# A fused decoder layer: q and k by tiles of 128 tokens across batch borders, with the engines' orders written out

## The chip, the cores and the metric

One core of a Trainium2 chip runs the whole layer in one launch. The metric is the device time of that launch in microseconds. The core has five engines that run beside each other and meet at semaphores: TensorE (PE, matmuls), VectorE (DVE), ScalarE (ACT), GpSimd (POOL) and SyncE (SP), which here only issues DMAs.

## The reference

32 batches of T = 112 tokens, model width M = 256, H = 8 heads of D = 128, a context of S = 375 rows per batch, FFN width F = 1024. Cut to what matters:

```
def attn(x, wq, wk, wv, wo):                     # x is layer-normed
    q, k, v = (einsum('bim,mhd->bhid', x, w) for w in (wq, wk, wv))
    q, k = rope(rmsnorm(q)), rope(rmsnorm(k))    # per head, over d
    s = (q * mult) @ (k * mult).T - 1e30 * later_keys
    return einsum('bhid,hdm->bim', softmax(s) @ v, wo)

x = x + attn(layernorm(x), wq, wk, wv, wo)
x = x + gelu(layernorm(x) @ ctx.T) @ ctx         # context of its own for each batch
x = x + quantised_ffn(layernorm(x), w1, b1, w2, b2)
```

The q and k projections treat each token by itself; only the rotary table depends on a token's place in its batch. Scores need all of a batch's q and k with D on the partitions.

## The kernel before

A batch's 112 tokens sit on 112 partitions. Each engine runs one loop, `body(i)`, whose order of work is written by hand; batches are pipelined over its iterations, so that one body of PE projects batch i+3, scores i+2 and finishes i-3.

The path of one batch's q and k: `stats_x`, `normalise_x` (DVE) and `root_x` (POOL) give the normed rows; `round_xn` (ACT) and `split_xn` (DVE) give them as a high and a low half in fp16; `transpose_x` (SP, a DMA transpose) puts M on the partitions. `project_q` and `project_k` (PE) do 12 matmuls each of 512 columns (two chunks of M, high x high, high x low, low x high, two banks), `project_v0` and `project_v1` 6 each. `square_q`, `square_k` (ACT) and `sum_squares_*` (DVE) give the RMS sums, `turn_cos_*`, `turn_sin_*` (DVE, straight from PSUM) the two products of the rotation, added by `turn_q` (DVE) and `turn_k` (POOL). ACT's `round_q0/1` scales and rounds q's high half, and `split_q` (DVE) makes its low half, one instruction per head:

```
for h in range(H):
    last = dve.scalar_tensor_tensor(out=qk16[:, 0, 1, at], in0=turn_c[:, 0, at], scalar=rms[:, 0, h:h + 1],
                                    in1=qk16[:, 0, 0, at], op0=ALU.mult, op1=ALU.subtract)
```

k goes by `scale_k0/1` and `round_k0` (ACT) and `split_k` (DVE). `transpose_q` and `transpose_k` (SP) each move 112 x 2048 fp16 values to `qkT`. Then `scores` (PE), `softmax_exp` (ACT), `mask_later_keys` (POOL), `weigh_values` (PE, P times V with a column of constants that gives the row sums), `invert_sums` (DVE), `normalise_o0/1`, `round_o` (ACT), `split_o` (DVE), `transpose_o` (SP), `project_out0` to `3` (PE), the residual, and the context and FFN parts in the same manner (`ctx_hidden`, `ctx_out`, `hidden_units0/1`, `out_units` on PE).

SP's queue holds every DMA of the kernel in one order; a wait in it holds back all that follow. PSUM has eight banks, and all are shared in turn: q's banks 3 and 4 also take part of o, k's banks 0 and 1 the scores.

## Time and profile before

| | us |
|---|---|
| three runs, median | 654.1 |
| three runs, lowest and highest | 652.81, 654.41 |
| the profiled execution | 654.7 |
| its span in the profile | 652.9 |
| of the span, PE busy | 593.3 |
| DVE busy | 588.1 |
| ACT busy | 543.0 |
| POOL busy | 348.0 |

The span runs from the first instruction of the program to the last; the time is what the device reports for the launch. Busy time of an engine counts each moment once, though its instructions overlap a little at their ends.

### The profile page before, as it was taken

To read this page: it belongs to the slowest core of one execution; us is meant where nothing else is said; L and a number is where in the kernel's file an instruction comes from. 1 tells how busy PE (TensorE), PEld (TensorE's weight loads), DVE (VectorE), ACT (ScalarE), POOL (GpSimd) and SP (SyncE) were. 2 spreads that over 40 slices of the span, in tenths; PEclk is the share of its full clock that TensorE was granted. 3 is DMA by queue.
4 is the path that set the end of the run, shared out by engine and by line. 5 is a ranking of instruction groups with operands and counts; after the bars stand their busy time and mean duration, and the time that the engine had idled before them with its cause. 6 is when DMAs were issued, how large, how long until landed. Compare 5 with 4: busy or idle time off the path is not lost.

```text
span 652.9 us, 13103 instructions
## 1 busy us (share of the span) xinstructions
PE 593.3 (91%) x4624; PEld 477.3 (73%) x4624; DVE 588.1 (90%) x1339; ACT 543.0 (83%) x1402; POOL 348.0 (53%) x430
## 2 busy tenths in 40 slices
PE   1746889999999999999999999999999999997864
PEld 1424667777887788888778877888887788776753
DVE  3768899999999999999999999999999999998442
ACT  6675788999999999989998899999889999998522
POOL 1134555665555565666655555656666555556111
PEclk9967999999999999999999999999999999999978
DMA  8071566766776766667687676666677777666451
GB/s 296 0 200 36 114 139 138 137 138 150 149 148 137 147 133 142 141 141 153 133 151 152 143 152 138 137 142 132 143 149 138 150 152 146 134 141 138 89 109 37
DMA packets 222641, 88.92 MB, mean 136 GB/s; under 512 B 200704, under 2 KB 217552, under 8 KB 222320
## 3 DMA queue, kind: packets, MB, share of 16 engines
q1 hardware_dynamic: 222576, 88.08, 63.6%
q8 instruction: 37, 0.61, 0.4%
q14 instruction: 28, 0.23, 0.1%
HBM read 34.84 MB, written 3.67 MB: 59 GB/s over the span
## 4 chain that ended last, share of the span: by engine, by line
DVE 75%; ACT 9%; PE 5%; POOL 3%; issue 3%; DMA 3%; SPq 0%; ACTq 0%; DVEq 0%
DVE turn_s L433 11%; DVE turn_c L425 8%; DVE qk L524 8%; DVE o L550 5%; DVE ss L566 5%; DVE turn_c L614 5%; DVE ss L603 5%; DVE qk L639 4%; DVE h_t L590 2%; DVE y_out L545 2%; DVE g L628 2%; DVE x L634 2%; DVE stat L534 1%; POOL turn_c L354 1%; DVE xn L600 1%
## 5 line engine op out<-in xcount | busy, mean ns | idle before, releaser
L912 PE MATMUL psum<-wqkv,xT 128*112 128x512 f16 x384 | 148.3, 386 | 12.5 <-DMA xT<-xn 9.1
L913 PE MATMUL psum<-wqkv,xT 128*112 128x512 f16 x384 | 147.4, 384 | 0.0
L914 PE MATMUL psum<-wqkv,xT 128*112 128x512 f16 x384 | 147.1, 383 | 0.0
L354 POOL TENSOR_TENSOR turn_c<-turn_c,turn_s 112x1024 f32<-112x1024 f32 x32 | 75.7, 2365 | 48.4 <-DVE turn_s L433 48.4
L912 PEld LDWEIGHTS psum<-wqkv,xT 128*112 128x112 f16 x384 | 50.7, 132 | 43.4 <-DMA xT<-xn 9.7
L425 DVE TENSOR_TENSOR turn_c<-psum,cos_t 112x1024 f32<-112x1024 f32 x64 | 77.8, 1215 | 0.0
L433 DVE TENSOR_TENSOR turn_s<-psum,sin_t 112x1024 f32<-112x1024 f32 x64 | 77.7, 1214 | 0.0
L914 PEld LDWEIGHTS psum<-wqkv,xT 128*112 128x112 f16 x384 | 50.7, 132 | 34.1 <-issue 1.9
L922 PE MATMUL psum<-wo,oT 128*112 128x256 f16 x256 | 71.0, 277 | 4.7 <-DMA oT<-o 3.5
L524 DVE SCALAR_TENSOR_TENSOR qk<-turn_c,rms,qk 112x128 f16<-112x128 f32 x256 | 69.2, 343 | 2.6 <-ACT qk L796 2.5
L924 PE MATMUL psum<-wo,oT 128*112 128x256 f16 x256 | 71.0, 277 | 0.0
L923 PE MATMUL psum<-wo,oT 128*112 128x256 f16 x256 | 71.0, 277 | 0.0
L913 PEld LDWEIGHTS psum<-wqkv,xT 128*112 128x112 f16 x384 | 50.7, 132 | 27.6 <-issue 1.3
L385 POOL TENSOR_TENSOR ve<-mv,ln_eps 112x1 f32<-112x1 f32 x32 | 6.6, 205 | 109.1 <-DVE mv L518 109.1
L1051 PE MATMUL psum<-v_sb,p_sb 112*112 112x129 f32 x512 | 62.1, 273 | 0.5 <-DVE turn_s L433 0.5
L1051 PEld LDWEIGHTS psum<-v_sb,p_sb 112*112 112x112 f32 x512 | 58.9, 176 | 0.9 <-POOL p_sb L368 0.9
L346 POOL TENSOR_TENSOR x3b<-x,b_rows 112x256 f32<-112x256 f32 x32 | 48.3, 1509 | 16.5 <-DVE y_out L545 13.2
L362 POOL TENSOR_TENSOR rms<-ms,nhalf 112x8 f32<-112x8 f32 x32 | 55.1, 1723 | 2.5
L381 POOL TENSOR_TENSOR rms<-ms,nhalf 112x8 f32<-112x8 f32 x32 | 53.3, 1665 | 2.5
L341 POOL TENSOR_TENSOR ve<-mv,ln_eps 112x1 f32<-112x1 f32 x32 | 9.2, 287 | 81.0 <-DVE mv L537 81.0
L1013 PE MATMUL psum<-qkT 128*112 128x112 f16 x256 | 42.6, 218 | 10.0 <-DVE turn_s L433 9.7
L961 PE MATMUL psum<-ctx_in,g 125*112 125x256 f32 x192 | 48.6, 390 | 3.3 <-ACT v_sb L708 3.3
(107 smaller groups left out, 1699.2 us busy)
## 6 DMA issues: line engine op xcount, KB each, us to landing
ctxT<-in_ctx_cols SPq DMA_DIRECT2D x32, 375.0 KB, 3.4
ctx_in<-in_ctx_rows SPq DMA_DIRECT2D x32, 375.0 KB
x_in<-in_x SPq DMA_DIRECT2D x32, 112.0 KB, 2.3
out_y<-y_out SPq DMA_DIRECT2D x32, 112.0 KB, 2.9
w_raw<-in_w SPq DMA_DIRECT2D x2, 1024.0 KB, 6.1
w_raw<-in_wk SPq DMA_DIRECT2D x2, 512.0 KB, 5.0
w_raw<-in_wq SPq DMA_DIRECT2D x2, 512.0 KB, 6.5
w_raw<-in_wv SPq DMA_DIRECT2D x2, 512.0 KB, 8.2
```

What stands on the lines that cost most here:

```text
L354: pool.tensor_tensor(turn_c[:, 1, :], turn_c[:, 1, :], turn_s[:, 1, :], ALU.add).then_inc(k_turned, 1)
L362: pool.tensor_tensor(rms[:, 1, :], ms[:, 1, :], nhalf[0:T, 0:H], ALU.pow).then_inc(k_rms_done, 1)
L425: return dve.tensor_tensor(turn_c[:, w, :].rearrange("t (b h d) -> t b h d", b=2, d=D), ps.rearrange("t b (h d) -> t b h d", d=D), cos_t[: ...
L433: return dve.tensor_tensor(turn_s[:, w, :].rearrange("t (h two f) -> t h two f", two=2, f=HALF), halves, table, ALU.mult)
L524: last = dve.scalar_tensor_tensor(out=qk16[:, 0, 1, at], in0=turn_c[:, 0, at], scalar=rms[:, 0, h:h + 1], in1=qk16[:, 0, 0, at], op0=ALU.m ...
L912: pe.matmul(dst, hi, wqkv[:, 0, c, w, cols], start=c == 0, stop=False)
L913: pe.matmul(dst, hi, wqkv[:, 1, c, w, cols], start=False, stop=False)
L914: last = pe.matmul(dst, lo, wqkv[:, 0, c, w, cols], start=False, stop=c == MC - 1)
L922: pe.matmul(y_ps, oT16[:, h, :], wo16[:, 0, h, :], start=first and h == heads[0], stop=False)
L923: pe.matmul(y_ps, oT16[:, h, :], wo16[:, 1, h, :], start=False, stop=False)
L924: product = pe.matmul(y_ps, oT16[:, H + h, :], wo16[:, 0, h, :], start=False, stop=last and h == heads[-1])
L1051: last = pe.matmul(o_ps[:, h // OH, at:at + VW], p_sb[:, h * T:(h + 1) * T], v_sb[:, h, :], start=h % OH == 0, stop=h % OH == OH - 1 or h ...
```

## The change

Eight batches of 112 tokens are 896 = 7 x 128 tokens. q and k are computed for 28 tiles of 128 consecutive tokens, whatever batch they belong to, in place of 32 batches of 112. A group is eight batches and seven tiles; `has_tile()` is false for every eighth batch, and in its place nothing of the x, q and k path is issued. Tile j of a group holds the last 112 - 16 j rows of batch j first (`own_rows`), then the first rows of batch j + 1. So `transpose_q` moves the rows of batch j to their place in `qkT`, and `transpose_q_next` the rest to the other buffer, in one DMA or two (`pieces_after`: a piece begins at partition 0, 32, 64 or 96, and rows that it takes too many land in a pad of 16 columns); k likewise. `qkT` has two buffers, `xT16` holds a group of seven tiles, the rotary tables have a row per token of a group (the cosine one only half as wide), and x is loaded a second time by tiles (`load_rows`). v is still projected per batch, now in the body of its scores (`project_v0/1` on columns of `xT16` that can lie in two tiles). q's low half is still made head by head from the rotated q, for 28 tiles. Some buffers share their room (`kn` with the raw weights, `on` and `p_sb` with the raw wo), and the PSUM banks are given out anew. Weights are prepared in another order, with a semaphore for each.

The order of each engine is new. It is now a `start()` and an `end()` of single calls and a `body(i)` for i = 5 to 25 between them.

```
+def done_t(j):
+    return (GROUP - 1) * (j.off // GROUP) + min(j.off % GROUP + 1, GROUP - 1)
...
+    def own_rows(j):
+        own = (P - T) * (j.off % GROUP)
+        return own, T - own
+    def pieces_after(cut):
+        a = cut // 32 * 32
+        return ((32, 64), (64, P)) if a == 32 else ((a, P),)
...
-                sp.dma_start_transpose(qkT[:, 0], qk16[:, 0].rearrange("t l n -> t (l n)")).then_inc(qT_landed, 16)
+                sp.wait_ge(q_lo_done, done_t(j))
+                own, cut = own_rows(j)
+                sp.dma_start_transpose(qkT[:, j.off % 2, 0, :, PAD + own:PAD + T], qk16[0:cut, 0].rearrange("t l n -> t (l n)")).then_inc(qT_landed, 16)
+            def transpose_q_next(j):
...
+                for a, b in pieces_after(cut):
+                    sp.dma_start_transpose(qkT[:, (j.off + 1) % 2, 0, :, PAD + a - cut:PAD + b - cut],
+                                           qk16[a:b, 0].rearrange("t l n -> t (l n)")).then_inc(qT_next_landed, 16)
...
-            def turn_cos(w, ps):
+            def turn_cos(w, ps, r):
+                table = cos_t[:, r, :].unsqueeze(1).broadcast_to([P, 2 * H, HALF])
...
-            def project(w, n, dst, j):
+            def project(w, n, dst, cols_of_x):
...
-                    hi, lo = xT16[:, c, :], xT16[:, MC + c, :]
+                    hi, lo = xT16[:, c, cols_of_x], xT16[:, MC + c, cols_of_x]
...
+            def scores(j):
+                pe.wait_ge(kT_landed, 16 * done_t(j))
+                pe.wait_ge(qT_landed, 16 * done_t(j))
...
+                if j.has(1):
+                    pe.wait_ge(qT_next_landed, next_landed(j.plus(-1)))
...
             def body(i):
-                a, b, c, d, e, f, g = (Batch(i + 3), Batch(i + 2), Batch(i + 1), Batch(i - 0), Batch(i - 1), Batch(i - 2), Batch(i - 3))
...
+                b, d, f, g, h = (Batch(i + 2), Batch(i - 0), Batch(i - 2), Batch(i - 3), Batch(i - 4))
+                project_out1(f)
+                project_out2(f)
+                project_out3(f)
+                project_out0(f)
+                project_v1(d)
+                ctx_out(g)
+                if b.has_tile():
+                    project_k(b)
+                hidden_units0(h)
+                scores(d)
+                project_v0(d)
+                transpose_xn2(f)
+                hidden_units1(h)
+                if b.has_tile():
+                    project_q(b)
+                ctx_hidden(f)
+                weigh_values(d)
+                out_units(h)
```

DVE's body of the change runs one place ahead of PE's (its g is i-3 where PE's f is i-2). On DVE the place is in the middle of the run, around the two products of k's rotation (`turn_c<-psum,cos_t` at L425, the first of the two, and `turn_s<-psum,sin_t`). Before, in every body:

```order
L550 TENSOR_TENSOR o<-on,o 112x1024 [waits o_hi_done]
L425 TENSOR_TENSOR turn_c<-psum,cos_t 112x1024 [waits k_squared]
L433 TENSOR_TENSOR turn_s<-psum,sin_t 112x1024
L563 SCALAR_TENSOR_TENSOR x<-psum,x 112x256 [waits x3b_done,ctxout_ready]
L566 TENSOR_REDUCE ss<-sq 112x8
L425 TENSOR_TENSOR turn_c<-psum,cos_t 112x1024 [waits q_squared]
L576 TENSOR_SCALAR xn<-x_in,mv,rstd 112x256 [waits x_rstd_done]
L581 BN_STATS stat<-x 112x6 [waits x3_done]
```

And now, in a group's seventh body (i = 6, 14, 22), where the tile whose k would be turned is missing:

```order
L848 TENSOR_TENSOR turn_c<-turn_c,turn_s 128x1024 [waits q_cos_done,q_sin_done]
L852 TENSOR_SCALAR xn<-x,mv,rstd 112x256 [waits x2_rstd_done]
L856 TENSOR_TENSOR qk<-w_raw,qk 128x1024 [waits k_hi0_done]
L860 TENSOR_SCALAR xn<-x_rows,mv,rstd 128x256 [waits x_rstd_done]
L874 BN_STATS stat<-x 112x6 [waits x3_done]
L876 MEMSET wait_cell 1x1 [waits x3_bn_done]
L877 BN_AGGR mv<-stat 112x2
L879 TENSOR_SCALAR ve<-mv 112x1 [waits x3_mv_done]
L895 TENSOR_SCALAR f_q<-f_int 128x448 [waits f0_int_done]
L900 TENSOR_SCALAR xq_int<-x,mv,rstd 112x256 [waits x3_rstd_done]
L904 TENSOR_SCALAR f_q<-f_int 128x448 [waits f1_int_done]
```

In a body with all tiles, k's sum of squares (L865), its sine product (L758) and its cosine product (L751) stand between `xn<-x_rows` and the statistics at L874 and behind them; they are gone from this body, q's sum of squares too, while q's addition (L848) and k's low half (L856) are still there. These two, with q's products and q's low half, are missing in the body after it.

On SP's queue, before, one body of the middle of the run (`qkT<-qk` is k's transpose at L266 and q's at L275, `oT<-o` is o's):

```order
L266 DMA_TRANSPOSE qkT<-qk 128x16x112 [waits k_lo_done]
L271 DMA out_y<-y_out 112x256
L275 DMA_TRANSPOSE qkT<-qk 128x16x112 [waits q_lo_done]
L279 DMA_TRANSPOSE oT<-o 128x16x112 [waits o_lo_done]
L282 DMA ctx_in<-in_ctx_rows 125x768
L289 DMA_TRANSPOSE xT<-xn 128x4x112 [waits v1_ready,xn_lo_done]
L250 DMA ctxT<-in_ctx_cols 128x2x375
L255 DMA_TRANSPOSE xqT<-xq 128x2x112 [waits xq_done]
```

And now, in a group's fifth body (k of tile 5 at L359 and L367 in the end of it, q of tile 4 at L329 and L337):

```order
L318 DMA_TRANSPOSE xqT<-xq 128x2x112 [waits xq_done]
L323 DMA ctxT<-in_ctx_cols 128x2x375 [waits h_ready]
L329 DMA_TRANSPOSE qkT<-qk 128x16x48 [waits q_lo_done]
L337 DMA_TRANSPOSE qkT<-qk 128x16x32 [waits q_lo_done]
L337 DMA_TRANSPOSE qkT<-qk 128x16x64
L343 DMA ctx_all<-in_ctx_rows 125x768 [waits ctxout_ready]
L348 DMA out_y<-y_out 112x256 [waits out_done]
L354 DMA_TRANSPOSE oT<-o 128x16x112 [waits y0_added,o_lo_done]
L359 DMA_TRANSPOSE qkT<-qk 128x16x32 [waits k_lo_done]
L367 DMA_TRANSPOSE qkT<-qk 128x16x32 [waits k_lo_done,s_ready]
L367 DMA_TRANSPOSE qkT<-qk 128x16x64
```

Between two context loads there stood two transposes for q and k, and there are now six, the last of them 16 to 64 rows wide; a store now waits for its result before o's transpose can be issued.

## Rows read from the trace of the kernel before

**Rows 1.** The page: busy us, share of the span and instructions of each engine.

```profile
PE 593.3 (91%) x4624; PEld 477.3 (73%) x4624; DVE 588.1 (90%) x1339; ACT 543.0 (83%) x1402; POOL 348.0 (53%) x430
```

**Rows 2.** Windows: us; busy PE, PEld, DVE, ACT, POOL; PEclk; DMA share; GB/s.

```profile
0.00:113.80 113.80, 74.41 (x463) 53.02 (x464) 86.20 (x160) 81.02 (x170) 45.97 (x64) 0.93 0.53 132
113.80:580.60 466.80, 466.35 (x3747) 379.32 (x3746) 462.30 (x1066) 424.02 (x1121) 281.48 (x338) 1.00 0.69 143
580.60:614.50 33.90, 29.37 (x248) 24.78 (x246) 25.10 (x65) 24.35 (x67) 14.53 (x17) 0.95 0.69 138
614.50:652.90 38.40, 23.20 (x175) 20.18 (x172) 14.55 (x50) 13.65 (x47) 6.07 (x11) 0.83 0.29 65
```

**Rows 3.** Timeline of PE, one body: start us, us, what it does.

```profile
302.12 0.21 PE L1013 MATMUL psum<-qkT 128*112 128x112 f16 x1
...
305.95 0.27 PE L922 MATMUL psum<-wo,oT 128*112 128x256 f16 x1
...
308.57 1.94 PE L1051 MATMUL psum<-v_sb,p_sb 112*112 112x129 f32 x16
310.35 1.04 PE L938 MATMUL psum<-w2T,f_q 128*112 128x256 bf16 x8
311.22 0.38 PE L912 MATMUL psum<-wqkv,xT 128*112 128x512 f16 x1
...
316.40 1.46 PE L961 MATMUL psum<-ctx_in,g 125*112 125x256 f32 x6
...
320.04 0.21 PE L1013 MATMUL psum<-qkT 128*112 128x112 f16 x1
```

**Rows 4.** Timeline of DVE, the same body.

```profile
299.45 1.22 DVE L433 TENSOR_TENSOR turn_s<-psum,sin_t 112x1024 f32<-112x1024 f32 x1
300.58 0.41 DVE L563 SCALAR_TENSOR_TENSOR x<-psum,x 112x256 f32<-112x256 f32 x1
...
311.83 2.15 DVE L524 SCALAR_TENSOR_TENSOR qk<-turn_c,rms,qk 112x128 f16<-112x128 f32 x8
313.91 0.41 DVE L530 TENSOR_SCALAR xn<-x,mv,rstd 112x256 f32<-112x256 f32 x1
...
317.38 1.22 DVE L433 TENSOR_TENSOR turn_s<-psum,sin_t 112x1024 f32<-112x1024 f32 x1
```

**Rows 5.** Two tiles' weight loads: min/median/max ns, first and last start.

```profile
L981 PEld LDWEIGHTS psum<-xqT,w1T x256: 95/97/152, 120.7 to 646.2; 128*128 128x128 bf16 x128
...
L912 PEld LDWEIGHTS psum<-wqkv,xT x384: 126/130/217, 17.4 to 592.4; 128*112 128x112 f16 x192
```

**Rows 6.** Groups by line, DVE: the split of the projection weights.

```profile
L455 DVE SCALAR_TENSOR_TENSOR wqkv<-w_raw,w_lift,wqkv 128x1024 f16<-128x1024 f32 x6 | 7.4, 1281 | 0.2
```

**Rows 7.** Timeline of ACT, four heads of o divided.

```profile
311.41 1.14 ACT L803 ACTIVATE on<-psum,rden 112x128 f32<-112x128 f32 x4
```

**Rows 8.** Timeline of SP's queue: one body's DMA issues.

```profile
306.19 1.20 SPq L289 DMA_TRANSPOSE xT<-xn  x1
...
310.52 0.58 SPq L262 DMA_DIRECT2D x_in<-in_x  x1
...
313.09 1.11 SPq L271 DMA_DIRECT2D out_y<-y_out  x1
314.25 1.90 SPq L275 DMA_TRANSPOSE qkT<-qk  x1
```

**Rows 9.** Tile xqT: issue of xq's transpose (ns), and us from issue to landing.

```profile
L255 SPq DMA_TRANSPOSE xqT<-xq x32: 1166/1167/1562, 112.3 to 643.6; - x32
...
DMA to landing us min/median/max: 2.3/2.3/6.2
```

**Rows 10.** Waits of SP's queue: us in total, times, longest.

```profile
SPq L288 <- PE psum L914: 161.9, 31, 15.9
```

**Rows 11.** Tile qkT: the same as rows 9 for q's transpose.

```profile
L275 SPq DMA_TRANSPOSE qkT<-qk x32: 1299/1754/3080, 44.5 to 600.7; - x32
...
DMA to landing us min/median/max: 4.0/4.4/6.5
```

More of the change, by code:

```diff
@@ L315, in _ @@
+            start()
+            for i in range(5, B - 6):
                 body(i)
+            end()
             for s in range(SLOTS):
@@ L412, in _ @@
+            start()
+            for i in range(5, B - 6):
                 body(i)
+            end()
         @block.vector
@@ L702, in _ @@
+            start()
+            for i in range(5, B - 6):
                 body(i)
+            end()
         @block.scalar
@@ L888, in _ @@
+            start()
+            for i in range(5, B - 6):
                 body(i)
+            end()
         @block.tensor
@@ L1093, in _ @@
+            start()
+            for i in range(5, B - 6):
                 body(i)
+            end()
 def tables_of(T, D):
```

2138 lines of the change are left out of this document (1537 added, 601 removed).

## The prediction

> **What bounds the kernel now.** I read the page's busy shares first. TensorE (PE) and VectorE (DVE) are both busy for about nine tenths of the span, ScalarE (ACT) for 83%, GpSimd (POOL) for 53% [rows 1]. So the shares alone don't say which engine it is. The windows cut the run into four stretches at two moments, the start of batch 5's k projection and that of batch 31's [rows 2]. The middle one, 466.8 us for 26 loop bodies, has PE busy for 466.35 us: the run is 113.8 us of filling, 26 bodies of 17.95 us, and 72.3 us of draining.
>
> Inside one body I look at starts, not at durations, since a matmul's time overlaps its successor's. PE's scores start at 302.12 and again at 320.04: 17.92 us, and the pieces between follow each other without a hole [rows 3]. The 24 matmuls for q and k take 316.40 - 311.22 = 5.18 us (0.216 each), those of the output projection 2.62 (305.95 to 308.57), P times V 1.78, the last FFN product 0.87. The six matmuls of one v half are 6 x 0.216 = 1.29. The granted clock there is 1.00, so this is PE at its real pace. On DVE one body runs from 299.45 to 317.38, 17.93 us, also without a hole: an operation over 1024 columns starts 1.13 after its predecessor, and the eight that give q's low half take 313.91 - 311.83 = 2.08 [rows 4]. The two engines are level. The chain of waits names DVE because it is a hair slower; a faster DVE alone would give nothing, nor would a faster PE. A change must take from both.
>
> **What the change removes.** Four of 32 q/k tiles. An instruction costs by its columns on both engines, and these don't change: 512 per matmul, 1024 per DVE operation. No row has one of these forms at 112 and at 128 partitions, so I bound it. On PE the loads of 128 x 128 for the FFN take 97 ns, those of 112 columns for q and k 130 [rows 5]: full width isn't dearer, below 0 there is nothing to gain since loads are hidden, so 0. On DVE the split of the weights, 128 x 1024 with a scalar per partition, has a mean of 1281 ns against the 1.22 us of one 112 x 1024 operation [rows 4, 6]: 0 to 5% more. I take 0, since that form also has the scalar; the 5% is rival E.
>
> PE loses 4 x 5.18 = 20.7 us: 32 x 17.92 = 573.4 becomes 552.7. DVE loses per tile eight operations of 1.13 (two cosines, two sines, two sums of squares, q's addition, k's low half), 2.08 for q's low half and about 1.2 for the statistics and rounding of x: 12.3 us, 4 x 12.3 = 49 in all, so its mean body is 17.93 - 1.54 = 16.4 against PE's 17.92 - 0.65 = 17.27. DVE stops being level; PE is the bound. ACT and POOL, below both, lose as well. q's low half head by head is no new work: the kernel before has those eight operations per batch [rows 4], now there are 28 x 8 in place of 32 x 8.
>
> **Does the saving arrive.** Seven bodies of eight still hold a full tile and one holds none of it, so means are not enough. On PE the body that would project tile 7 takes 17.92 - 5.18 = 12.74. DVE body i+1 runs beside PE body i (its first operations need what that PE body has just produced). DVE's k part of the missing tile (3 x 1.13 for k, 1.13 for q's sum, 4.52) falls out of exactly the DVE body beside the light PE body: 13.4 against 12.74. The next DVE body lacks another 6.6 and waits for PE. So the light pair costs 13.4, not 12.7, and its neighbours stay at 17.92. The tightest loop between the two is: P times V ends, DVE inverts the sums, ACT divides the eight heads (two halves of 1.14, and a tanh over 336 columns between them, about half of one: 2.8) [rows 7], the context product in PE's next body waits for that. From that product to the end of P times V PE has 17.92 - 2.62 - 1.29 - 0.87 = 13.1, and 13.1 + 0.2 + 2.8 + some semaphore steps of 0.1 = 16.4, under 17.92 by 1.5. In the light body this slack is short by up to 1.2. I put 4 us for these things over the loop.
>
> **The queue that is moved past.** SP issues all DMAs in order. Before, it issues nine per body; xT costs it 1.20, x 0.58, a store 1.11, q 1.90 [rows 8], xq 1.17 [rows 9]. It waited 161.9 us for v1_ready alone [rows 10], so it has room. Now each tile's q and k are cut at the batch border, into two pieces, and for tiles 4 and 5 of a group into three, and there is one row load more: per eight batches 16 + 16 pieces in place of 8 + 8. Eight bodies then cost: xq 1.17, o 1.9 (as q), x 0.58, a store 1.11 and the two context loads (as an x load and a store, 0.58 + 1.11), 8 x 6.45 = 51.6; xT 7 x 1.20 = 8.4; the row loads 7 x 0.58 = 4.1; 32 pieces at 1.8 = 57.6. Together 121.7, 15.2 per body, under 17.27. What a piece of 16 to 64 rows costs to issue no row shows; the smallest transpose issues in 1.17, q's take from 1.30 to 3.08 [rows 9, 11]. I take 1.8, the median of q's 1.75 rounded up, the nearest form. A body with three pieces for q and three for k comes to 6.45 + 1.2 + 6 x 1.8 = 18.5, over 17.9; behind them queue the context load, a store, o's transpose (what PE's output projection waits for) and k's. They are late by 1 to 2 us and catch up in the two short bodies that follow; part of the 4 us is theirs. The traffic itself grows little if it goes by rows: q and k now move 960 rows per group and not 896, 7% more. The DMA engines are busy 69% of the middle stretch [rows 2]; even if all of it were q and k in 4% less time, they would be at 77%.
>
> A rule stands against this edit. The rows first: a transpose of 112 x 256 lands 2.3 us after its issue, one of 112 x 2048 in 4.4 [rows 9, 11], so 2 us of each are there whatever the size, while the next issue starts after 1.2 to 1.9 us. By the rows only issue counts, and the sum is the 121.7 above. The Trainium skill ("DMA: Bandwidth & Descriptors", Rules for kernel authors) says of two transfers to disjoint partition halves that one shouldn't bother, as they serialize, and to use one 128-partition transfer. If the fixed 2 us of the 16 extra pieces were serial, the sum would be 51.6 + 8.4 + 4.1 + 28.8 + 32 = 124.9, still below 138.2; the trace's successive issues without a landing between them [rows 8] don't bear the rule out, and rival C is the form in which it would bite.
>
> **Start and end.** Both are now written out and not cut from the loop's body. Count PE's work: before, by 113.8 it had done 573.4 - 26 x 17.92 - 44.4 = 63 (44.4 is what is left at 580.6, counted in the pieces of rows 3). So the start costs 51 us over its work, the end 72.3 - 44.4 = 28. Of the end's, 38.4 us run after the last P times V [rows 2]: o's normalisation, its transposed landing, two layer norms, the FFN. That chain is the same in the new kernel.
>
> New start: by PE body 5 it has done 81 us of work. DVE's share of that opening is 90 us (five q tiles, six k tiles, seven of x, and 12 of weight preparation). In the first 113.8 us DVE idles 27.6 [rows 2]; with as much idle DVE reaches its body 5 at 117, PE 13 later, at 130: overhead 49, so 2 less. It starts worse (project_k(0) now stands behind all four weight sums and behind wo) and fills better (no body of 17 us per batch for half-empty stages). New end: batches 30 and 31 both live on tile 30, and 73 us of PE work are left when that tile is projected, as long as the chain behind it. So PE idles only behind the last P times V: 38.4 less some 21 us of work there is 17; I take 20 for 28, 8 less.
>
> **Sum, against the profiled span.** 652.9 - 20.7 (PE's matmuls) - 2 (start) - 8 (end) + 4 (light bodies, three-piece tiles) = 626 us. The profiled execution's time was 654.7, 1.8 over its span, and the median of the three runs 0.6 under that: I predict **627 us**, 4% faster. For this forecast: start +-8, end 17 to 28, stalls 2 to 12, hence 614 to 640.
>
> **Rivals.**
> A, the forecast: 0.70.
> B, PE's light bodies are swallowed: q pieces land late, ACT waits for them before it overwrites qk, and each group gives back its 5.2 us (less the 0.65 that a lighter DVE body leaves). 3 x 4.5 in the loop for the 4 of the sum, and 0.15 more in each of 26 bodies: 640. For it: the tight 1.5 us of slack and three pieces in a row. Against: the light bodies coincide. 0.14.
> C, slower: SP's queue becomes the bound. The place is the pieces' issue; at price c the eight bodies take 64.1 + 32c, equal to before's 143.4 at c = 2.48. At 2.6 it is 147.3, 1.1 us a body more than forecast, 26 bodies: 30 us, 657. For it: q's issue has reached 3.08 when it stood right behind another large one [rows 11], which is now the rule. Against: the median of 1.8. 0.06, of which 0.02 within 0.3%. (The Trainium skill's rule above, read as every piece waiting for the landing before it, is this case.)
> D, more: DVE idles 15 and not 27 in the opening: 614. 0.07.
> E, DVE's tile operations cost 5% more at 128 partitions. Its mean body would still be hidden (16.9), but a full body is level with PE's: 5% of 11.1 us is 0.55 on seven of eight bodies, 12 us over 26: 639. 0.03.
>
> The range 614 to 643 takes in E and most of B; beyond it lie C, parts of D and B and the forecast's own tails, 0.2 in all. Within 0.3% (2 us, about what a measurement of this kernel can tell from no change) lies 0.02, slower 0.04, faster 0.94.
>
> **What would show it.** The profile after should have q/k matmuls at the same 0.216 us from start to start; a period of 138 to 140 us per eight bodies of PE, with one of 13 to 14 among 17.9s; DVE busy near 540 us with holes; PE's idle in the loop behind DMA landings or ACT's o small. If SPq shows issues of q and k pieces over 2.4, C is right; if PE waits for qkT or for DVE in the light bodies, B. The prediction is wrong if 128 partitions cost DVE more than 5% over 112, if the opening takes longer than 140, or if the small transposes land later than 5 us.

## The result, and the profile after

The changed kernel takes 679.57 us (median of four runs, 677.15 to 680.94), the kernel before beside it 654.25: a ratio of 1.0387, with a 95% interval of 1.0353 to 1.0421. It is 3.9% slower. The forecast was 627 us and faster, with a range up to 643: wrong in its sign. The profiled execution has a span of 677.4 us. Where a later kernel had runs more than 1.5% above its fastest, its time is that of the others.

The page of the changed kernel: busy times (beside [rows 1]), the DMA queue's share of the 16 engines' time, and the chain that ended last.

```profile
PE 584.7 (86%) x4528; PEld 442.2 (65%) x4528; DVE 562.0 (83%) x1255; ACT 498.2 (74%) x1322; POOL 352.3 (52%) x402
...
q1 hardware_dynamic: 236656, 94.43, 76.7%
...
DVE 36%; PE 20%; SPq 20%; ACT 4%; POOL 4%; DMA 4%; issue 4%; ACTq 0%; DVEq 0%
```

Every engine but POOL was busy for less time than before, and yet the span grew. So the loss is waiting, and the chain names where: a fifth of it is SyncE's queue, which in the kernel before had 0%. POOL too has fewer operations, 402 for 430; that it is busy for 352.3 us and not less than 348.0 means that some of them became longer, and the next part shows which.

To compare loops I use one event, the start of the last FFN product of a body (`out_units`), and 21 bodies from the first of them. The windows of the changed kernel, cut there (columns as in [rows 2]):

```profile
0.00:134.80 134.80, 96.63 (x586) 60.76 (x587) 109.38 (x204) 99.03 (x216) 66.27 (x80) 0.94 0.68 145
134.80:534.60 399.80, 367.31 (x2954) 283.92 (x2952) 354.92 (x807) 308.46 (x849) 234.36 (x255) 1.00 0.87 146
534.60:604.30 69.70, 59.99 (x445) 44.58 (x446) 59.83 (x127) 50.27 (x139) 34.38 (x40) 0.95 0.72 133
```

In the loop PE works 367.3 of 399.8 us and DVE 354.9: neither is level with the loop any more, unlike in [rows 2]. The DMA engines' share there is 0.87, not the 0.77 that the prediction gave as its ceiling. Bodies 7 to 17, from start to start: 17.9, 19.4, 19.5, 19.5, 19.5, 17.9, 17.4, 19.7, 17.9, 19.4, 19.5 us. The 17.4 is the light one that should have been 13.4, and four of eight bodies are 1.6 us longer than the 17.92 at which they were to stay. The forecast gives these 21 bodies 18 x 17.92, 3 x 13.4 and its 4 us of stalls, 366.8 us in all; they took 33 more. PE began body 5 at 135.7 and not at 130, which is 6 us. Of the 51 us between the two spans (677.4 and 626.2) that leaves 12 for the end.

**The 19.5 us bodies.** One of them on DVE (start, us, what), with what it waited for in brackets:

```profile
237.16 0.40 DVE L843 SCALAR_TENSOR_TENSOR x<-psum,x 112x256 f32<-112x256 f32 x1
237.48 1.21 DVE L848 TENSOR_TENSOR turn_c<-turn_c,turn_s 128x1024 f32<-128x1024 f32 x1
239.40 0.41 DVE L852 TENSOR_SCALAR xn<-x,mv,rstd 112x256 f32<-112x256 f32 x1 [0.71 <-POOL rstd L577]
239.73 1.22 DVE L856 TENSOR_TENSOR qk<-w_raw,qk 128x1024 f16<-128x1024 f32 x1
240.86 1.22 DVE L860 TENSOR_SCALAR xn<-x_rows,mv,rstd 128x256 f32<-128x256 f32 x1
242.00 1.21 DVE L865 TENSOR_REDUCE ss<-sq 128x8 f32<-128x1024 f32 x1
```

and GpSimd (POOL) at the same time:

```profile
237.32 1.42 POOL L575 TENSOR_TENSOR ve<-mv,ln_eps 112x1 f32<-112x1 f32 x1 [1.79 <-DVE mv L837]
238.82 0.55 POOL L577 TENSOR_TENSOR rstd<-ve,nhalf 112x1 f32<-112x1 f32 x1
...
240.95 0.98 POOL L583 TENSOR_SCALAR_AFFINE_SELECT wo_raw<-wo_raw 112x896 f32<-112x896 f32 x1
```

Read the ends. POOL's addition of one element per partition (L575) takes 1.42 us and ends at 238.74, when DVE's `turn_q` (L848) ends at 238.69; in the kernel before the same addition takes 0.19 to 0.21 in all 32 cases. DVE's `normalise_x2` then waits 0.71 for the square root behind it. And `normalise_x` (L860) takes 1.22 us and ends at 242.08, just behind POOL's mask (L583, to 241.93); in the kernel before `normalise_x` takes 0.40 to 0.42 in all 32 cases. Sum: 0.71 + 0.82 = 1.53 of the 1.6 us. The rest of the trace says the same: the addition takes 1.42 us in all 17 bodies in which `turn_q` runs beside it, and mostly 0.19 and at most 1.08 in the others. `normalise_x` takes 1.21 to 1.22 in all nine in which the whole mask runs beside it, and 0.40 to 0.41 in the loop's others; these nine are the loop's nine bodies of 19.4 and 19.5 us. By the records `normalise_x` starts 0.09 us before the mask that holds it (240.86 and 240.95), when `split_k` ahead of it ends at 240.95: which of two began first can't be read from such starts. A third pair costs nothing here: GpSimd's `turn_k` takes 4.11 us beside DVE's eight operations for q's low half (247.58 and 247.29), 2.35 without them, and does so in the orders below whose full bodies take 17.9 us too. The operations with one operand in PSUM, and those of DVE alone, kept their durations at 128 partitions (1.21 to 1.22), and the q and k matmuls follow each other by 0.216 us (236.91, 237.13).

**The queue.** SyncE in the changed kernel, a body with a tile in three pieces (L337 is q's piece for the next batch, L343 the context load, L354 o's transpose):

```profile
289.49 0.57 SPq L323 DMA_DIRECT2D ctxT<-in_ctx_cols  x1
290.11 1.21 SPq L329 DMA_TRANSPOSE qkT<-qk  x1
291.36 2.68 SPq L337 DMA_TRANSPOSE qkT<-qk  x2
294.09 1.22 SPq L343 DMA_DIRECT2D ctx_all<-in_ctx_rows  x1
295.35 0.35 SPq L348 DMA_DIRECT2D out_y<-y_out  x1
295.80 4.21 SPq L354 DMA_TRANSPOSE oT<-o  x1
300.06 1.22 SPq L359 DMA_TRANSPOSE qkT<-qk  x1
301.38 2.13 SPq L367 DMA_TRANSPOSE qkT<-qk  x1
303.56 0.76 SPq L373 DMA_DIRECT2D x_in<-in_x  x1
304.37 1.40 SPq L308 DMA_DIRECT2D x_rows<-in_x  x1
```

There is no gap. A row's length here is the time until the next can be issued, and o's transpose takes 4.21; before, its own took 2.09 (median between 160 and 520 us) and q's of the same size 1.75 [rows 11]. Tile oT of the changed kernel between 160 and 520 us, issue in ns and landing in us:

```profile
L354 SPq DMA_TRANSPOSE oT<-o x19: 1527/4024/4885, 163.5 to 501.4; - x19
...
DMA to landing us min/median/max: 4.0/7.1/8.6
```

### The profile page after: what moved, and what is told of

It reads as the page before. It is cut to its first block, busy times and chain, and to the rows that moved or that the text cites. A ratio compares the mean times of both kernels' runs of the same rounds, so it can differ in the third digit from the quotient of the medians.

```text
span 677.4 us, 13174 instructions
## 1 busy us (share of the span) xinstructions
PE 584.7 (86%) x4528; PEld 442.2 (65%) x4528; DVE 562.0 (83%) x1255; ACT 498.2 (74%) x1322; POOL 352.3 (52%) x402
## 4 chain that ended last, share of the span: by engine, by line
DVE 36%; PE 20%; SPq 20%; ACT 4%; POOL 4%; DMA 4%; issue 4%; ACTq 0%; DVEq 0%
DVE turn_c L751 5%; DVE turn_s L758 5%; SPq L354 4%; SPq L367 4%; DVE qk L922 4%; SPq L337 3%; POOL ve L575 3%; DVE qk L856 3%; PE psum L1749 3%; PE psum L1750 3%; DVE o L830 3%; PE psum L1901 3%; PE psum L1751 2%; DVE ss L865 2%; DVE ss L942 2%
## 5 line engine op out<-in xcount | busy, mean ns | idle before, releaser
L1749 PE MATMUL psum<-wqkv,xT 128*128 128x512 f16 (+1 forms) x352 | 139.0, 395 | 19.0 <-DMA xT<-xn 6.3
L1750 PE MATMUL psum<-wqkv,xT 128*128 128x512 f16 (+1 forms) x352 | 138.4, 393 | 0.0
L1751 PE MATMUL psum<-wqkv,xT 128*128 128x512 f16 (+1 forms) x352 | 137.7, 391 | 0.0
L603 POOL TENSOR_TENSOR turn_c<-turn_c,turn_s 128x1024 f32<-128x1024 f32 x28 | 90.4, 3227 | 16.8 <-DVE turn_s L758 13.2
L1901 PE MATMUL psum<-v_sb,wo_raw 112*112 112x129 f32 x512 | 62.9, 275 | 16.1 <-DVE turn_c L751 13.0
L1749 PEld LDWEIGHTS psum<-wqkv,xT 128*128 128x128 f16 (+1 forms) x352 | 39.7, 113 | 54.4 <-issue 11.3
L1901 PEld LDWEIGHTS psum<-v_sb,wo_raw 112*112 112x112 f32 x512 | 58.7, 176 | 18.9 <-issue 18.5
L751 DVE TENSOR_TENSOR turn_c<-psum,cos_t 128x1024 f32<-128x1024 f32 x56 | 68.0, 1215 | 0.5 <-ACT sq L1398 0.3
L758 DVE TENSOR_TENSOR turn_s<-psum,sin_t 128x1024 f32<-128x1024 f32 x56 | 67.9, 1212 | 0.0
L922 DVE SCALAR_TENSOR_TENSOR qk<-turn_c,rms,qk 128x128 f16<-128x128 f32 x224 | 64.6, 359 | 3.6 <-ACT qk L1392 1.7
L1751 PEld LDWEIGHTS psum<-wqkv,xT 128*128 128x128 f16 (+1 forms) x352 | 39.6, 113 | 40.8 <-issue 5.8
L575 POOL TENSOR_TENSOR ve<-mv,ln_eps 112x1 f32<-112x1 f32 x32 | 30.6, 956 | 63.8 <-DVE mv L837 63.8
L1750 PEld LDWEIGHTS psum<-wqkv,xT 128*128 128x128 f16 (+1 forms) x352 | 39.6, 113 | 31.6 <-issue 4.5
L1799 PE MATMUL psum<-ctx_all,g 125*112 125x256 f32 x192 | 48.0, 386 | 9.4 <-DVE g L964 7.3
L571 POOL TENSOR_TENSOR rms<-ms,nhalf 128x8 f32<-128x8 f32 x28 | 48.7, 1738 | 2.2
```

Source lines behind the costliest of these rows:

```text
L603: pool.tensor_tensor(turn_c[:, 1, :], turn_c[:, 1, :], turn_s[:, 1, :], ALU.add).then_inc(k_turned, 1)
L751: return dve.tensor_tensor(turn_c[:, w, :].rearrange("t (h f) -> t h f", f=HALF), ps.rearrange("t b (h f) -> t (b h) f", f=HALF), table, A ...
L758: return dve.tensor_tensor(turn_s[:, w, :].rearrange("t (h two f) -> t h two f", two=2, f=HALF), halves, table, ALU.mult)
L1749: pe.matmul(dst, hi, wqkv[:, 0, c, w, cols], start=c == 0, stop=False)
L1750: pe.matmul(dst, hi, wqkv[:, 1, c, w, cols], start=False, stop=False)
L1751: last = pe.matmul(dst, lo, wqkv[:, 0, c, w, cols], start=False, stop=c == MC - 1)
```

## The experiments

Two theories stood after this reading. T1: DVE and GpSimd exclude each other in certain pairs of operations, and the new order of DVE's body makes such pairs meet. T2: the queue, with more and dearer transposes. All differences below are against the kernel named; the kernel before took 654.1 to 654.8 us beside each group. "Loop" is the 21 bodies, "eight bodies" bodies 8 to 15 and 16 to 23.

### DVE's order: three kernels

**normalise_x early.**

```diff
                 if d.has_tile():
                     turn_q(d)
+                if b.has_tile():
+                    normalise_x(b)
                 normalise_x2(g)
                 if d.has_tile():
                     split_k(d)
-                if b.has_tile():
-                    normalise_x(b)
```

> One part undone of the order on VectorE: in the loop's body normalise_x of tile i+2 runs between turn_q and normalise_x2, no longer behind split_k. Everything else is the changed kernel. Theory T1 (VectorE and GpSimd exclude each other in some pairs of operations): in a full body normalise_x ran while GpSimd had its mask of p and took 1.22 us in place of 0.40, and turn_q held GpSimd's small addition for the variance, so that normalise_x2 waited 0.7 us. Moved, normalise_x fills that wait and stands clear of the mask: a full body of 19.53 us becomes about 18.4, and some 13 full bodies give 13 to 15 us, so the time is 662 to 667 us. Theory T2 (SyncE's queue and the transposes that land late are the cause): VectorE's order matters nothing, the body stays at 19.5 and the time at 678 to 681 us. By the theory that 128 partitions cost VectorE more, nothing changes either.

Measured: 673.53 us (1.0276 of before, 1.0244 to 1.0308), 6 less than the changed kernel. The full bodies do what T1 says, 18.5 in place of 19.5, and `normalise_x` has a median of 408 ns where it had 1214. The light body does the opposite: 19.1 in place of 17.4. Eight bodies: 147.7 and 149.7, for 150.8 and 152.9. Something else holds the group at some 148 to 150, and the time missed T1's 662 to 667 us.

**Both pairs apart.**

```diff
                 split_o(f)
-                stats_x2(g)
-                residual_ctx(h)
                 if d.has_tile():
                     turn_q(d)
+                stats_x2(g)
+                residual_ctx(h)
+                if c.has_tile():
+                    sum_squares_k(c)
                 normalise_x2(g)
-                if d.has_tile():
-                    split_k(d)
                 if b.has_tile():
                     normalise_x(b)
+                if d.has_tile():
+                    split_k(d)
                 if c.has_tile():
-                    sum_squares_k(c)
                     turn_sin_k(c)
```

> VectorE's body in another order, the same operations: split_o, turn_q, stats_x2, residual_ctx, sum_squares_k, normalise_x2, normalise_x, split_k, turn_sin_k. So GpSimd's small addition for the variance has VectorE's residual addition and a sum of squares beside it and no operation on two SBUF inputs from another tile, and normalise_x no longer falls under the mask. Theory T1: both losses go, 0.82 us of normalise_x and 0.71 us of waiting; a full body falls from 19.53 to 17.9 to 18.1 us, PE and VectorE level again, and the loop's full bodies give 18 to 21 us: 658 to 662 us. Theory T2: within 2 us of the changed kernel, 678 to 681 us, because the queue is unchanged. If VectorE's dearer bodies were a symptom of DMAs, the duration of normalise_x would stay 1.2 us wherever it stands.

Measured: 677.45 us (1.0336, 1.0297 to 1.0376). The mechanism is as T1 expected: full bodies 17.9, POOL's addition in the new place (ns, min/median/max)

```profile
L575 POOL TENSOR_TENSOR ve<-mv,ln_eps x19: 189/189/1077, 179.4 to 514.6; 112x1 f32<-112x1 f32 x19
```

for a median of 1420 in the changed kernel. The time is T2's: 2 us less than the changed kernel, which lies within the spread of either's runs. The bodies around the three-piece tiles take 18.8, 19.0, 20.7 in place of 19.5, 17.9, 17.4, and eight take 148.2 and 150.0 again. SyncE's waits over this kernel's loop, all of them:

```profile
SPq L359 <- DVE qk L856: 13.2, 4, 4.4
SPq L354 <- DVE o L830: 10.0, 3, 3.3
SPq L353 <- PE psum L1760: 2.6, 3, 0.9
SPq L312 <- DVE xn L909: 2.2, 2, 1.2
```

28 us in 393. The 161.9 us for v1 in the kernel before [rows 10] are of the whole run, with one wait of 15.9; between 150 and 520 us it was

```profile
SPq L288 <- PE psum L914: 92.8, 20, 5.1
```

and with its two other waits 119.6 in 370. SyncE's room is nearly gone; whether it is the bound is tested below by taking load from it.

**The mask for one head.** GpSimd's mask does 112 columns in place of 896.

```diff
-                p = p_sb.rearrange("k (h t) -> k h t", h=H)
+                p = p_sb.rearrange("k (h t) -> k h t", h=H)[:, 0:1]
-                                   pattern=[[0, H], [1, T]], channel_multiplier=-1)
+                                   pattern=[[0, 1], [1, T]], channel_multiplier=-1)
```

> The changed kernel with GpSimd's causal mask applied to head 0 only (112 columns in place of 896; seven heads stay unmasked, so seven eighths of this operation's work is left out). All orders are those of the changed kernel. Theory T1, exclusion: the mask takes some 0.2 us, normalise_x in the full bodies falls from 1.22 to at most 0.5 us, a full body from 19.53 to 18.7 to 18.8 (the 0.71 us that VectorE waits for GpSimd's variance stay), and the time from 679.6 to 671 to 674 us, as the queue becomes the bound. If normalise_x's 1.22 us have another reason (the operand x_rows, a DMA that writes beside it), they stay, and the time is 676 to 680 us.

Measured: 673.60 us (1.0307, 1.0278 to 1.0337); full bodies 18.7. `normalise_x`, in its old place:

```profile
L860 DVE TENSOR_SCALAR xn<-x_rows,mv,rstd x18: 400/407/524, 161.8 to 516.9; 128x256 f32<-128x256 f32 x18
```

No order on DVE was touched; GpSimd's work alone made it 0.8 us longer, and the addition beside the untouched `turn_q` kept its 1.42. T1 is shown.

### The context load's place: six kernels that made it worse

**Context load behind k's pieces.**

```diff
-                load_ctx(f)
                 store_out(i)
                 transpose_o(e)
                 if c.has_tile():
                     transpose_k(c)
                     transpose_k_next(c)
+                load_ctx(f)
                 load_x(d)
```

> SyncE's body in another order, the same DMAs: the context load of 375 KB for batch i-2 is issued behind the transposes of o and k, and no longer ahead of the store and of o's transpose. Theory T2: o's transpose no longer queues behind 375 KB, so it takes 2 us to issue and lands 4.5 us later (now 3.5 and 6.8), the light bodies fall from 17.4 to 14 to 15 us and the long ones behind three-piece tiles from 19.7 and 22.3 to 18 to 19.5: 8 to 12 us, 668 to 672 us. Theory T1: the full bodies are VectorE's and stay at 19.53 us; what the queue gives back is at most the 2 to 4 us of the long bodies, 675 to 678 us. If context arrives too late instead, ScalarE or PE waits for ctx_landed and the time rises above 682 us.

Measured: 697.56 us (1.0648, 1.0621 to 1.0675), 18 more. o's transpose does issue in 1.53 and land in 4.2. But now x's rows stand behind the 375 KB: their landing goes from 2.3 to 5.5 us, and DVE waits for them 16 us between 200 and 500 (9 before this edit). That is part of the 11 us by which the loop grew; the rest wasn't traced. The local claim held, the consequence didn't.

**The same with the second kernel's DVE order.**

> Both edits together: VectorE's order of the second kernel and SyncE's order of the third. Theory T1 with T2 as a second, separate cause: the gains add, 18 to 21 us and 4 to 12 us: 648 to 658 us. If both act on the same waits, it is no more than 2 us under the better of the two alone. If T1 alone is right, it equals the kernel with VectorE's order, 658 to 662 us. 627 us, the forecast, is out of reach of all of them, since the opening (6 us) and the end (11 us) are longer than forecast, whatever the loop does.

Measured: 706.32 us (1.0783, 1.0744 to 1.0822). The two edits together gain nothing, and the bodies that had been 17.9 are 19.6 to 20.4 us.

**Context load first in the body** (with the second order).

```diff
+                load_ctx(f)
                 if a.has_tile():
                     load_rows(a)
...
-                load_ctx(f)
                 store_out(i)
```

> VectorE's order of the second kernel (split_o, turn_q, stats_x2, ...), and SyncE's body with load_ctx(i-2) issued first and no longer between the q pieces and the store. In the second kernel full bodies took 17.9 us, but SyncE waited only 28 us in 370 and o's transpose, behind the 375 KB context load, took 4.25 us to issue. Theory Q (the order on the queue: o's transpose stands behind a large load): its issue falls to 1.6 us and its landing from 7.5 to 4.2, and unlike in the third kernel the context is there earlier and not later, so the bodies of 18.8, 19.0 and 20.7 us in each group shrink to 18 or less: 12 to 15 us less than the second kernel, 662 to 665 us. Theory F (the DMA system is full: whatever stands behind the load waits the same): the 2.7 us come back at other issues, and the time stays within 3 us of 677 us.

Measured: 711.97 us (1.0879, 1.0829 to 1.0928). Neither theory had this. Between 150 and 520 us, a wait of DVE:

```profile
DVE stat L957 <- DMA x_rows<-in_x: 41.4, 13, 6.0
```

In the second kernel it was 13.0. x's rows are loaded in the same body in which DVE reads them, and now land in 5.5 us.

**The plain loads on ScalarE's queue** (with the second order).

```diff
-    (SyncE's body) load_rows(a), load_ctxT(f), load_ctx(f), load_x(d)
+    (ScalarE's body) load_ctx(f) behind relu0, load_rows(a) behind round_xn,
+                     load_ctxT(f) behind relu1, load_x(d) at the end
```

> VectorE's order of the second kernel, and in the loop's body the four plain loads (context twice, x, the tile's rows) are issued by ScalarE on its own DMA queue; SyncE keeps the transposes and the store. Nothing is left out. Theory N: SyncE loses 0.73 + 0.58 + 0.91 + 0.43 = 2.65 us of issue per body and the 2.7 us that o's transpose stands behind the context load, so its 18.5 us per body fall under 15 and PE and VectorE are the bound: 650 to 658 us, unless ScalarE, busy 74%, loses as much by issuing them (2.65 us of 17.9, where it has 4.6 free): then 660 to 665 us. Theory B: the DMA engines have the same to move, and the time stays at 672 to 678 us, with transposes that take longer to issue or to land.

Measured: 696.64 us, with 687.1 for the profiled one (1.0676, 1.0605 to 1.0747). Tile oT of this kernel, who waited for it and its landing:

```profile
  PEld psum L1774: 20.6, 6
  PE psum L1774: 19.1, 6
...
DMA to landing us min/median/max: 4.0/6.9/13.9
```

The issue became cheap (median 1.55) and the longest landing went from 9.2 to 13.9 us (the median from 7.5 to 6.9); k's transposes land in some 6 us for 4. The DMA engines' share was 0.92. As I read it, large loads from another queue move at the same time as the urgent transposes, and the one queue's order had kept them apart; no run separates this from the time that ScalarE spends on issuing.

**Behind the rows' load, and behind the other context load** (on the kernel with a pad of 48, below).

> The best real version so far (normalise_x early, no tile in three pieces, 667 us), with the context load of 384 KB issued second in SyncE's body, right behind the rows' load, and no longer ahead of the store and o's transpose. Queue-order theory: o's transpose issues in 1.6 and lands in 4.2 us in place of 4.2 and 7.3, the rows' load isn't delayed as it was with the context load first, and the bodies of 19.1 and 16.8 shrink: 655 to 662 us. Against it: what now stands behind the load, x's transpose and x_q's, lands 3 us later, and PE waits for k's or the FFN's input: then 675 to 700 us, as in the two earlier kernels that moved this load.

Measured: 680.70 us (1.0415, 1.0363 to 1.0468), 14 more than its base. x's transpose lands in 6.1 us for 3.1, and bodies of 22.4 and 26.3 us appear.

> As the kernel before it in this call, but with the context load right behind the other context load and ahead of q's pieces. Queue-order theory: o's transpose then has q's pieces between itself and 768 KB of loads; it issues in 2 to 3 us, q's pieces take what it took before, 2 to 3 us more to issue; their consumer, the scores, comes 9 us later in PE's body, so the time is 658 to 666 us. Traffic theory: within 3 us of 667 us. Above 675 us if q's pieces, late by 3 us, hold up ScalarE's next q.

Measured: 680.4 us (1.0401, 1.0312 to 1.0489), the mean of 675.7 and 685.1. q's pieces for the next batch issue in 4.35 us and land in 6.9 (medians). At five other places the load was never better than at its own: what stands right behind it landed some 3 us later in four of them, and the fifth was ScalarE's queue.

### How much the queue has to carry: four kernels

**Whole tiles, 14 transposes of q and k in place of 32.**

```diff
-                own, cut = own_rows(j)
-                sp.dma_start_transpose(qkT[:, j.off % 2, 0, :, PAD + own:PAD + T], qk16[0:cut, 0]...
+                sp.dma_start_transpose(qkT[:, j.off % 2, 0, :, 0:PAD + T], qk16[:, 0]...
(k alike; no transpose_q_next, transpose_k_next, and no waits for them)
```

> VectorE's order of the second kernel, and q and k of a tile each transposed by one instruction over all 128 rows into the tile's own buffer; the pieces for the next batch and the waits for them are left out (so scores of most batches read wrong rows). 14 transposes of q and k per eight batches in place of 32, and 896 rows in place of 960. Theory N (the number of instructions on the queue costs): 18 issues of 1.3 to 1.8 us less are 23 to 32 us of SyncE's 148 per eight bodies, PE and VectorE are the bound again at 139 to 141 us, and the time is 650 to 655 us. Theory B (the rows moved cost, by the DMA engines): q and k move 7% less, all transposes together some 4% less, 142 to 146 us per eight bodies: 668 to 673 us.

Measured: 653.53 us (0.9982, 0.9954 to 1.0010), 24 less than the second kernel: its loop is 17 us shorter and its end 10. The time is theory N's; eight bodies take 141.6 and 141.9, between N's 139 to 141 and B's 142 to 146. With the pieces it also leaves out the waits for them, so it doesn't tell the queue's load from pieces that land late.

**As many transposes, fewer rows.**

```diff
-                for a, b in pieces_after(cut):
+                for a, b in pieces_after(cut) if j.off < 5 else [(a, a + 16) for a, b in pieces_after(cut)]:
```

> VectorE's order of the second kernel, the same number of transposes, but from tile 5 on each piece for the next batch moves 16 rows only (9 pieces of 16 in place of 512 rows per q and per k and group, 592 rows in place of 960; the rest of the rows is left out and the scores read old ones). The counterpart of the kernel with whole tiles: fewer rows, as many instructions. Theory N: SyncE's queue stays at 145 to 148 us per eight bodies, 672 to 677 us. Theory B: a third less q and k traffic, 139 to 141 us per eight bodies, 650 to 655 us.

Measured: 660.33 us (1.0091, 1.0064 to 1.0119), eight bodies 143.6 and 142.4. That is outside both ranges, 5 us over B's and 12 under N's. So the pair doesn't choose between N and B: either cut, in number or in rows, brings back most of the 7 us per eight bodies that the queue cost. What differs is the price of a packet: over 16 bodies the 256-byte packets of the transposes took 23.7 ns on average in the kernel before, 30.7 in the changed one, 25.7 with whole tiles and 31.1 here. Fewer transposes went with cheaper packets, fewer rows did not. But the number isn't all of it: with the context load behind k's pieces, above, the same 32 transposes had packets of 26.8 ns. What else sets that price wasn't tested.

**DVE's old order with whole tiles**, the fourth corner of a square.

> The kernel with whole-tile transposes (14 in place of 32 per eight batches, the pieces for the next batch left out), but with VectorE's order as in the changed kernel, not the second one's. The queue is relieved, the collisions of VectorE and GpSimd are back. With the other order this took 141.6 us per eight bodies. Theory T1: five bodies of eight are full on VectorE and cost 19.5 us again; their two or three neighbours give nothing back, so 141.6 becomes 149 to 151 us and the time 668 to 674 us. If the queue was the only real bound, the period stays at 141 to 143 us and the time at 652 to 656 us. The two together say how much of the 25 us over the forecast each cause holds when the other is gone.

Measured: 666.17 us (1.0189, 1.0137 to 1.0241), a little under the range given (two runs); eight bodies take 147.7 and 147.0. The loops' windows, in this order: kernel before; second DVE order with pieces; old order with whole tiles; second order with whole tiles (the old order with pieces is above).

```profile
131.20:508.00 376.80, 376.47 (x3027) 306.63 (x3026) 373.36 (x862) 342.01 (x904) 227.37 (x273) 1.00 0.69 143
```

```profile
133.60:526.60 393.00, 370.22 (x2954) 287.56 (x2953) 349.46 (x805) 309.49 (x849) 222.86 (x255) 0.99 0.89 148
```

```profile
135.00:524.00 389.00, 366.18 (x2954) 285.35 (x2953) 354.13 (x806) 308.28 (x849) 237.34 (x255) 1.00 0.77 146
```

```profile
132.60:508.70 376.10, 365.34 (x2955) 284.61 (x2953) 345.25 (x805) 308.00 (x849) 227.22 (x255) 1.00 0.80 151
```

From 376.1 the collisions alone add 12.9 us, the pieces alone 16.9, both together 23.7. They partly hide behind each other: in time, DVE's order mended alone gave 2 (6 with normalise_x alone), the queue alone 13, both 26. The windows are of single executions, and that of the corner with both mended was the fastest of eight, 3 us under its median; the three differences can be too large by that much.

**No tile in three pieces**, nothing left out (with normalise_x early).

```diff
-PAD = 16
+PAD = 48
...
-        return ((32, 64), (64, P)) if a == 32 else ((a, P),)
+        return ((0 if a == 32 else a, P),)
(and the semaphore counts to match)
```

> VectorE's order of the first kernel (normalise_x ahead of normalise_x2), and no tile in three pieces: where the cut is at 48 or 32 rows, the next batch's piece is one transpose of all 128 rows that begins 48 or 32 columns further left, in a pad of 48 columns in place of 16. Per eight batches 28 transposes of q and k in place of 32, and 1024 rows in place of 960. Nothing is left out. If the number of instructions is what costs, 4 issues of 1.5 us less bring the bodies behind those tiles down by 3 to 6 us per eight: 147.7 to 143 us, the time 658 to 666 us. If the rows cost as much, 64 rows more each for q and k (7%) eat it: 671 to 677 us against the first kernel's 673.5.

Measured: 666.94 us (1.0195, 1.0160 to 1.0229), 6.6 less than the kernel with normalise_x early; eight bodies 145.1 and 143.6. 4 transposes fewer are worth more than 64 rows of q and as many of k cost. It is the fastest kernel that leaves nothing out, and still slower than the kernel before.

### Splitting alone, in the kernel before: two kernels

```diff
-                sp.dma_start_transpose(qkT[:, 1], qk16[:, 1]...).then_inc(kT_landed, 16)
+                for r in (slice(0, 64), slice(64, T)):
+                    sp.dma_start_transpose(qkT[:, 1, :, r], qk16[r, 1]...).then_inc(kT_landed, 16)
(q alike)
```

> The kernel before, with one edit: each transpose of q and of k in two instructions, rows 0 to 64 and 64 to 112, so 32 in place of 16 per eight batches and not a row more. It puts the changed kernel's count of transposes into a kernel with room on its queue (SyncE waits some 6 us per body for v1_ready and others). If a split costs only an issue of 1.2 to 1.5 us, the queue takes it up and the time stays within 0.5% of 654.5 us. If a split also slows the moving itself (a 256-byte packet of a transpose took 23.7 ns in the kernel before and 30.7 in the changed one, 25.7 with whole tiles), packets rise to 28 ns or more here, the DMA engines' share from 0.70 to 0.80 or more, and o's transpose lands later: 658 to 668 us.

Measured: 697.86 us (1.0667, 1.0633 to 1.0702): 43.7 us more for not a row more, far over both expectations. One body of the chain that ended last:

```profile
315.45 1.24 SPq L277
316.73 5.99 DMA qkT<-qk
322.77 0.26 PE psum L1015
...
329.46 0.48 DVE x L636
329.95 1.15 DVE qk L641
331.11 1.24 SPq L267
332.39 1.92 SPq L267
334.36 1.14 SPq L272
335.55 1.24 SPq L277
336.83 5.90 DMA qkT<-qk
342.77 0.26 PE psum L1015
```

It is a closed loop: scores (L1015), ..., k's low half (L641), two issues for k (L267), the store (L272), two for q (L277), landing, scores. Between 150 and 520 us SyncE still waited 70 us for v1, so the queue was not full; the path through it had become too long. From k's first issue to q's last it takes 5.72 us (331.11 to 336.83), in the kernel before 3.00 (311.25 to 314.25), and the landing behind it 5.9 for some 4.4. Against these 4.2 us stood little slack: in the kernel before q had landed 1.4 us (median) before the scores began. From scores to scores this is 20.0 us.

```diff
-                if i.inside(B):
-                    store_out(i)
                 if c.inside(B):
                     transpose_q(c)
                 if d.inside(B):
                     transpose_o(d)
+                if i.inside(B):
+                    store_out(i)
```

> The kernel before with q and k transposed in two instructions each, as in the last run of that kind (698 us, 19.6 us a body), and the store of the output issued behind o's transpose and no longer between k's pieces and q's. Latency theory: that kernel is bound by a chain of one body, k's low half on VectorE, two issues for k, the store's issue of 1.16, two for q, q's landing of 4.6 to 6.0, the scores; the store leaves the chain, so a body gets 1.1 us shorter, 18.4 to 18.6, and the time is 668 to 674 us. Traffic theory (slower packets, the DMA engines): the same bytes in the same number of instructions, 695 to 700 us.

Measured: 682.84 us (1.0455, 1.0407 to 1.0503): 15 us less, 151 for eight bodies in place of 157. The same DMAs, so the traffic theory falls; the latency theory has the right sign and asked for 24 to 30. Of the store's 1.16 us on the path 0.6 to 0.8 came back per body; packets also took 27.4 ns here against 23.7, which may be the rest, and that isn't shown.

## Why the prediction was wrong, step by step

- **PE and DVE per operation**: right. 0.216 us per q/k matmul, 1.21 to 1.22 per DVE operation at 128 partitions; rival E is refuted.
- **"its neighbours stay at 17.92"**: the first step that failed. DVE's body was counted as a sum of rows, each at its own duration, and GpSimd was dismissed with "ACT and POOL, below both, lose as well". Each duration holds for the order in which it was read. In the new order two pairs meet on the path in nine of the loop's 21 bodies and make them 19.5; POOL lost nothing, 352.3 us busy for 348.0. Worth up to 12.9 us in the loop by itself. The trace before already had a sign of it, off the path, in GpSimd's addition `x3b`, of 256 columns:

```profile
L346 POOL TENSOR_TENSOR x3b<-x,b_rows x32: 722/1641/1799, 119.0 to 645.1; 112x256 f32<-112x256 f32 x32
```

It takes 0.72 to 0.73 us in the five batches without DVE's `split_o` beside it and 1.64 to 1.80 in the 27 with it. A rule of the Trainium skill ("SBUF — State Buffer", SBUF: two separate sides) describes it: VectorE and GpSimd share one pair of ports as an exclusive lock, against GpSimd for a VectorE operation in a two-port mode, or for one with two SBUF inputs if GpSimd's reads SBUF, and the loser is blocked for the whole instruction. By that rule the trace agrees for `turn_q` (two SBUF inputs): 1.42 for 0.19 us on GpSimd. `normalise_x` has one tensor input and would have to run in a two-port mode; no row says that it does, and at 0.32 us from start to start for 256 columns it isn't faster than `split_xn` with its two inputs. That it took 1.22 for 0.40, and in the loop only beside the whole mask, is measured either way.
- **"Together 121.7, 15.2 per body, under 17.27"**: the second. The pieces were priced well: 1.8 given, 1.6 to 1.8 on average measured, so rival C's price of 2.48 never came. The dear one was o's transpose, taken at about the 1.9 of q: 3.8 on average in the changed kernel and 4.3 with the second order. Other rows came cheaper (a store 0.35 for 1.11), so that SyncE's rows sum to 16.1 and 16.8 us per body (bodies 8 to 23), still under the 17.27. The rest of the error is in "under": a queue in order whose issues each wait for data of a certain moment can't use its gaps, and 16.8 us of issue went with bodies of 18.5. "It has room" rested on the 161.9 us of the whole run; in the loop the wait for v1 was 4.5 us per body. Rival C's outcome (SyncE the bound, slower) was thus the right rival with the wrong price; it had 0.06. Worth up to 16.9 us in the loop by itself; how it divides between the number of issues and the rows moved stays open.
- **"even if all of it were q and k in 4% less time, they would be at 77%"**: wrong, 0.87. Only the rows were scaled; a 256-byte packet's time rose from 23.7 to 30.7 ns.
- **Light body 13.4**: with both causes away it was 15.4, and the next 18.7: eight bodies 141.6 where 138 to 140 were forecast. This has the form of rival B's give-back, at 2.8 of the 4.5 us that it had per group, but without late pieces; its cause wasn't tested. In the changed kernel itself the light body took 17.4.
- **Start and end**: taken as 2 and 8 us less than before; 6 and 12 us longer than forecast. From the 22nd `out_units` on the changed kernel takes 142.8 us, with whole tiles 142.1 in the old order of DVE and 139.8 in the second, so the two causes explain at most 3 of the 12. Two more are a meeting of the same kind: at 549.5 us one `normalise_x` takes 2.43 us beside GpSimd's `turn_k`. The rest, and the start's 6, stay open; in the changed kernel PE is busy 59.99 of the first 69.7 us there.
- **What was to make it wrong**: 128 partitions dearer than 5%, an opening over 140, small transposes landing later than 5 us. None of the three happened (3.8 us for q's next pieces, median). The list looked only at the parts that were already in the sum.

With both causes away, and part of q's and k's work left out, the time was still 653.5 us, beyond the range. Its span, 648.5, is 22 over the forecast's 626.2: 3 in the start, 9 in the loop, in the light bodies and in the last one (21.8 us), and 10 in the end. So the two causes explain why the kernel was slower, and not the whole distance to the forecast.

## What to carry to other kernels

Where two engines can exclude each other, a duration in the profile belongs to an order: before a body is reordered, lay the new order's long VectorE operations with all inputs in SBUF beside GpSimd's, and price each meeting at up to the length of the partner. Compare each GpSimd operation's shortest and median time first: where they differ, as 722 and 1641 ns did here, a pair already meets. Price a DMA queue by what stands ahead of each urgent transfer, not by the mean, and treat a split transfer as a longer path first: with two more issues on a chain that had 1.4 us of slack, a queue that still waited 70 us cost 44. When two causes each hold a loop near the same length, test them in a square: either alone gave 2 to 13 us, both 26.

## What the hardware showed that was not expected

A transpose's issue is not a constant: 1.5 us for o's with room ahead of it, 4.7 (median, up to 5.5) right behind 375 KB and a store. Splitting q's and k's transposes raised the mean time of their 256-byte packets from 23.7 to 27.1 ns in the kernel before, without a row more. With the plain loads issued from ScalarE's queue the longest landing of o's transpose from SyncE's was 13.9 us, for 9.2. A GpSimd addition of one element per partition takes 1.42 us beside one VectorE operation, seven times its own 0.19.
